# Two 16-head attentions in one kernel: the score products of a batch in one row over four row groups, in front of its last transposes

## The reference, cut to what matters

```python
qh = qp.reshape(bsz, t, H, D).transpose(0, 2, 1, 3)      # H = 16 heads, D = 8
attn = jnp.einsum('bhtd,bhsd->bhts', qh, kh) * scale
attn = jax.nn.softmax(attn, axis=-1)
ctx = jnp.einsum('bhts,bhsd->bhtd', attn, vh)
out = ctx.transpose(0, 2, 1, 3).reshape(bsz, t, H * D) @ out_w.T + out_b
...
x = x + jnp.tanh(g_xattn[3]) * _L3_xattn_ref(_layernorm(x, axis=-1), ctx_1024, ctx_1024, ...)
```

## Time and profile before

| what | value |
|---|---|
| time, median of 3 runs | 643.35 us (641.51 to 653.01) |
| the profiled execution's own time | 643.2 us |
| span of its trace | 641.1 us |
| busy in the span: PE, PEld, DVE, ACT, POOL | 92%, 62%, 61%, 59%, 35% |
| mean granted PE clock | 0.954 of full speed |
| first attention, scores to last update of x | about 27 to 89 us of the span |
| second attention, the same | about 411 to 473 us of the span |

### The profile page before, as it was taken

One profiled execution on the slowest core, in us unless ns is written; L12 is line 12 of the kernel. 1 busy time (PEld: TensorE's weight loads), 2 busy tenths in 40 slices (PEclk: granted clock), 3 DMA queues, 4 the chain that ended last, 5 costly groups with the idle time before them and its releaser, 6 DMA issues.

```text
span 641.1 us, 10297 instructions
## 1 busy us (share of the span) xinstructions
PE 589.4 (92%) x3526; PEld 400.0 (62%) x3526; DVE 392.3 (61%) x739; ACT 375.5 (59%) x752; POOL 221.4 (35%) x209
## 2 busy tenths in 40 slices
PE   8999986999998998999897998899985899999997
PEld 6466754786664445776553444467753688888885
DVE  4578839464633346777145665388849566666665
ACT  4377774556644336888543444477773456666663
POOL 5007664581000000000000434000023288888884
PEclk9999988999988998999898999899987799999999
DMA  8200001340000000000000101000001256655550
GB/s 281 87 2 2 2 1 42 92 98 21 2 1 1 0 0 1 1 3 1 2 0 0 37 13 61 1 2 3 1 6 37 63 165 180 180 175 173 174 150 34
DMA packets 14850, 33.53 MB, mean 52 GB/s; under 512 B 2912, under 2 KB 8432, under 8 KB 14672
## 3 DMA queue, kind: packets, MB, share of 16 engines
q1 hardware_dynamic: 14800, 32.89, 17.3%
HBM read 32.03 MB, written 0.85 MB: 51 GB/s over the span
## 4 chain that ended last, share of the span: by engine, by line
PE 76%; DVE 8%; issue 8%; ACT 7%; POOL 2%; ACTq 0%; DVEq 0%; POOLq 0%
PE bank L726 8%; PE bank L727 8%; PE bank L728 8%; PE bank L643 5%; PE bank L654 4%; PE bank L669 3%; PE bank L957 3%; PE bank L617 3%; PE bank L608 3%; PE bank L572 2%; ACT wa L1266 2%; PE bank L1101 2%; PE bank L967 2%; PE bank L1126 2%; PE bank L1124 2%
## 5 line engine op out<-in xcount | busy, mean ns | idle before, releaser
L726 PE MATMUL bank<-xn_hi,w_hi 128*128 128x512 f32 x168 | 69.1, 411 | 14.1 <-DVE wc L1728 7.1
L453 POOL TENSOR_TENSOR h_lo<-wc,h_hi 128x512 fp32r<-128x512 f32 x56 | 72.4, 1296 | 19.8 <-ACT h_hi L1335 19.8
L728 PE MATMUL bank<-xn_hi,w_lo 128*128 128x512 f32 x168 | 68.4, 407 | 0.0
L727 PE MATMUL bank<-xn_lo,w_hi 128*128 128x512 f32 x168 | 68.3, 407 | 0.0
L1752 DVE TENSOR_TENSOR wb<-arena,bank 128x512 f32<-128x512 f32 x64 | 44.0, 687 | 33.3 <-PE bank L728 33.2
L1335 ACT ACTIVATE h_hi<-wc 128x512 fp32r<-128x512 f32 x56 | 35.4, 633 | 44.4 <-DVE wc L1760 29.8
L1547 DVE TENSOR_TENSOR wa<-bank,row_max 128x512 f32<-128x512 f32 x64 | 44.2, 691 | 7.5 <-ACT wb L1212 4.3
L1543 DVE TENSOR_REDUCE row_max<-bank 128x4 f32<-128x512 f32 x64 | 43.6, 681 | 8.1 <-PE bank L643 7.5
L1212 ACT ACTIVATE wb<-wa 128x512 f32<-128x512 f32 x64 | 40.1, 630 | 13.8 <-DVE wa L1547 13.4
L445 POOL TENSOR_TENSOR w_lo<-ring,w_hi 128x384 fp32r<-128x384 f32 x42 | 42.8, 1020 | 15.5 <-ACT w_hi L1312 15.5
L534 POOL TENSOR_TENSOR x<-x,upd 128x128 f32 x8 | 6.0, 753 | 120.6 <-ACT upd L1202 120.6
(11 more groups left out here) (286 smaller groups left out, 1307.8 us busy)
## 6 DMA issues: line engine op xcount, KB each, us to landing
arena<-comb_rows SPq DMA_DIRECT2D x64, 256.0 KB, 4.0
ring<-in_experts SPq DMA_DIRECT2D x42, 192.0 KB, 2.4
ring<-in_experts SPq DMA_DIRECT2D x8, 256.0 KB, 3.5
mats<-in_mats SPq DMA_DIRECT2D x1, 1472.0 KB, 9.7
mats<-in_mats SPq DMA_DIRECT2D x1, 832.0 KB, 5.5
mats<-in_mats SPq DMA_DIRECT2D x2, 320.0 KB, 7.8
x<-in_x_t SPq DMA_DIRECT2D x1, 512.0 KB, 4.1
context<-in_ctx_t SPq DMA_DIRECT2D x1, 512.0 KB, 4.8
```

The costliest lines, as they stand in the source:

```text
L453: nc.gpsimd.tensor_tensor(h_lo[:, v % 3, :], hidden_of(v), h_hi[:, v % 3, :].bitcast(f32), ALU.subtract).then_inc(m_h_lo, 1)
L726: mm(out, w, x_, start=start, stop=False)
L727: mm(out, w, x_rest, start=False, stop=False)
L728: return mm(out, w_rest, x_, start=False, stop=stop)
```

## The change

The two halves of a batch's scores become one row of sixteen products. In the new row the four row groups take turns product by product (block `m_` of units 0, 1, 2, 3, then the next block), where before two row groups took turns. The whole row stands where the second half stood: in front of the transposes of unit 3. The first half's place, in front of the transposes of unit 1, is empty. The wait of the whole row is the one the second half had: all four units of the batch before must be subtracted. DVE's, ACT's and POOL's streams are unchanged.

```diff
-                def scores(b, p):
-
-                    if b == 0 and p == 0:
+                def scores(b):
+
+                    if b == 0:
                         pe.wait_ge(a_q_rows, 8 * inst + 4)
                         pe.wait_ge(a_k_rows, 8 * inst + 8)
-                    if b == B // 2 and p == 0:
+                    else:
+                        pe.wait_ge(a_sub, base + 4 * b)
+                    if b == B // 2:
                         pe.wait_ge(a_q_rows, 8 * inst + 8)
-                    if b > 0:
-                        pe.wait_ge(a_sub, base + 4 * b + 2 * p - 2)
                     for m_ in range(QUADS):
-                        for i in range(2):
-                            r = 2 * p + i
+                        for r in range(4):
                             rows = slice(32 * r, 32 * r + 32)
...
-                scores(0, 0)
-                scores(0, 1)
+                scores(0)
                 q_rows_of(inst, 1)
                 pe.wait_ge(a_q_rows, 8 * inst + 8)
                 for b in range(B):
                     for u in range(4):
-                        if u % 2 == 1 and b + 1 < B:
-                            scores(b + 1, u // 2)
+                        if u == 3 and b + 1 < B:
+                            scores(b + 1)
                         transposes(b, u)
```

## The result

The changed kernel takes 659.25 us (median of 4 runs, 659.02 to 661.9), the kernel before 643.38 us. The ratio is 1.026, 95% interval 1.024 to 1.028: 15.9 us slower. The prediction was 657.0 us, range 647 to 667. The profiled execution took 661.9 us, with a span of 659.8 us and a mean clock of 0.941; it is the longest of the four, the other three had a mean clock of 0.949.

A forecast was written before the change was run, and what follows sets the result against it. The prediction took PE to bound the attention loops before, and a ring of waits of 7.72 us per batch after. Each attention ends 6.8 us later, both 13.7: 643.2 + 13.7 = 656.9, forecast 657.0 us, range 647 to 667.

The forecast's parts named there:

- PE bounds the loops before: In the attention loops of the kernel before, every step of a batch lies on PE, busy 45.87 of 46.00 us.
- A row of sixteen costs 1.09: On PE, sixteen score products with four row groups side by side take 1.09 us, as one half did.
- The bound of 1.65 and its rival: Score row on PE takes 1.65 us, no more overlap than two successive halves; total 664.7 us, chance 0.10.
- The ring: Per batch, scores wait for DVE's subtractions and division, which wait for scores: 7.67 us, through ACT 7.57, taken as 7.72.
- The first batch: At each attention's start, batch 0's row saves nothing; DVE's first maximum of batch 1 moves from 35.40 to 37.63.
- The forecast's 36.33: In the first batch, time when unit 2's transposes and unit 1's V products end and the row of batch 1 starts.
- The sum per attention: Batch 7's first maximum comes 7.12 us later, less 0.3 at the end: each attention ends 6.8 us later.
- The clock: Rival: PE's idle time in the new loop lets its clock fall in half of 14 rounds; 662.5 us, chance 0.20.
- The prediction's own sign of being wrong: In the changed loops, score rows following at 6.8 us or less, or a clock clearly below 1.00.
- The price of the falls: Clock falls in half of the 14 attention rounds cost 0.8 us each, 5.6 us in all.
- PE stays the bound: Rival: in the loops, PE's 15.3 us less work is gained in full; 627.9 us, chance 0.04.
- the ring closes faster: Rival: handing over between engines overlaps, so a batch takes 7.3 us; total 651.2 us, chance 0.11 for 7.3 or less.

The follow-up runs named there:

- halves_one_place: The changed kernel with the sixteen products in the old sequence, units 0 and 1 alternating, then units 2 and 3, in the new place: 657.75 us.
- filled_gap: The changed kernel with five unused products behind the V products of unit 2 each round and five in the gap beginning each attention: 655.72 us.
- first_only: The changed kernel with the change in the first attention alone, the second keeping two halves per batch: 654.92 us, ratio 1.015 to the kernel before.
- alternate_even: The changed kernel with batches 2, 4, 6 scored by a row before unit 2's transposes, odd batches by halves in old places, batch 0 by a row: 639.76 us.

## Why the prediction was right, and where its steps were off

- **PE bounds the loops before.** Right, 45.87 of 46.00 us. But freeing it was worth nothing in this place (halves_one_place), as the prediction said.
- **A row of sixteen costs 1.09.** Measured 1.11 (58.61 to 59.72). The bound of 1.65 and its rival are out, and four row groups here cost 0.02 us over two. By the Trainium skill (TensorE: Matmul & The Clock Gate, Measured speedup vs the span model) 1.15 was an estimate for it, 0.04 too long; the 0.11 us for one record that went into it stands in no row.
- **The ring.** Summed to 7.67 through DVE and 7.57 through ACT, taken as 7.72. Measured 7.66 over six batches of the first attention and 7.76 between the two rows shown; in the second at full clock (56.77 - 10.19) / 6 = 7.76 (filled_gap). Both ways exist: with the division out of the ring 7.45 is left, with both out 6.73. That the sum through DVE is so close is in part luck: row to first maximum was 1.19, not 1.30, and the four units took 5.48, not 5.37, since the 5.37 was read off batch 7, the shortest; the two errors cancel.
- **The first batch, mis-sized.** The step "The row of batch 0 saves nothing: DVE has time there until the query products are through" was wrong. The query products stand behind the row in PE's stream, and the first exp waits for them. In the changed kernel they start 1.10 us behind the first score product instead of 1.65:

```profile
26.79 1.17 PE L642 MATMUL bank<-arena 32*128 32x128 f32 x32 [0.69 <-ACT v_ones L1189]
27.89 3.70 PE L617 MATMUL bank<-xn,spread_w 128*128 128x512 f32 x8
```

  DVE's first maximum of batch 1 came at 10.16 instead of the forecast 37.63 - 26.77 = 10.86, so 0.7 us early, 0.55 of it from this row and 0.11 from the 1.19 instead of 1.30. The forecast's 36.33 holds 0.10 that its terms do not name: 35.29 + 0.58 + 0.36 = 36.23.
- **The sum per attention.** Forecast 2.2 (first batch) + 4.9 (six rounds) - 0.3 (end) = 6.8. Measured in the first attention 10.16 - 8.63 = 1.5, then 45.95 - 41.43 = 4.5, then -0.15: 5.9. In the second at full clock 6.8 (filled_gap). Together 12.7, forecast 13.7. The second attention's round is 0.1 us longer at the same clock because in its middle rounds DVE's four units take 5.56 us, not 5.48, and DVE waits 0.08 us more for L679 behind them (halves_one_place, at full clock in both attentions). The kernel before has the same difference in the units (5.55 and 5.47), hidden behind PE. What delays them is open.
- **The clock.** It was a rival with a chance of 0.20, and it happened: 659.25 - 655.7 = 3.5 us of the 15.9 are gone once both idle times are filled, and the mean clock rose from 0.949 (three of the four runs) to between 0.956 and 0.959. The prediction's own sign of being wrong, a clock of the loops clearly below 1.00, showed in the second attention. The price of the falls was put at 5.6. So the total was met in part by luck, because two errors had opposite signs: the attentions 1 us too long in the forecast, the clock left out of its likeliest case.
- **PE stays the bound; the ring closes faster.** Neither: DVE waits for scores in every batch.

The rule of the Trainium skill that the prediction weighed (TensorEngine Tiling (Array Packing), PSUM Bottleneck) came out true in its result, a faster PE and no gain. The trace is more exact than the rule, though: DVE had 26% of idle time. It was not the speed of the reader of the banks alone but the order of waits that bounded the loop, since the same row one unit earlier takes 6.73 us a batch.

## What to carry to other kernels

A step that gets cheaper by being bundled must also wait for all that its parts waited for. So before bundling, add up the ring from the bundled step through its consumers back to its wait, with everything that stands in front of it in its engine's stream, and compare it with the busiest engine's time per round; here that sum was right to 0.1 us, with two errors of 0.11 us that cancelled. If the ring is longer, the place counts more than the form: moving the same row one unit ahead took back the whole loss.

## What the hardware showed that I had not expected

The clock can stay low while the trace shows PE busy without a pause. In first_only PE was busy 14.00 of 14.00 us from 428 to 442; the clock was 0.50 up to 439.9 and 1.00 behind that, 0.57 on the mean. The Trainium skill (TensorE: Matmul & The Clock Gate, What's actually happening) says that activity releases the throttle; this stretch does not agree. Its section Seeing it yourself warns that the clock's records can be unreliable and that it has been seen stuck, at another level and for longer than here. The record is borne out here by a half's 2.01 us instead of 1.09. What lets it rise was not settled.

A fall can also hit code that was not changed. In first_only the second attention, whose code is that of the kernel before, took 5.9 us more behind a first attention that ended 5.9 us later, and with five small products in a gap of 1.4 us this was gone (medians 654.9 and 649.0 us). The same filler in alternate_even brought nothing, and four kernels with the gap unfilled had no fall there in their profiled executions, so the gap can be a condition of the fall but not its whole cause. Whether the later start plays a part was not tested.
